# First cross attention: the next unit's scores follow the last mix, the final turn and half of the maxima come behind them

## The reference

```python
q = _split_heads(x @ wq.T + bq, H)
k = _split_heads(mem @ wk.T + bk, H)
v = _split_heads(mem @ wv.T + bv, H)
scores = jnp.einsum('bhqd,bhkd->bhqk', q, k) * (1.0 / math.sqrt(hd))
attn = jax.nn.softmax(scores, axis=-1)
out = _merge_heads(jnp.einsum('bhqk,bhkd->bhqd', attn, v))
```

## Time and profile before

| what | us |
|---|---|
| median of three runs | 3806.73 (3805.34 to 3807.47) |
| the profiled execution, its own time | 3805.49 |
| the profiled execution, span of its instructions | 3803.7 |
| first cross attention, from about 300 to about 1195 of the span | about 895 |

### The profile page before, as it was taken

How to read it: one execution, slowest core, us unless ns; L and a number is a source line. 1 busy time by engine, 2 the same in 40 slices (tenths; PEclk the granted TensorE clock), 3 DMA queues, 4 the chain that set the end, 5 groups by cost and what they waited for, 6 DMA issues and landing times. The chain is left out here.

```text
span 3803.7 us, 68033 instructions
## 1 busy us (share of the span) xinstructions
PE 3376.3 (89%) x26619; PEld 1977.6 (52%) x26619; DVE 2561.0 (67%) x5544; ACT 1947.0 (51%) x2681; POOL 1538.7 (40%) x1207
## 2 busy tenths in 40 slices
PE   5769999999997579599999999999999999779998
PEld 3555665666654367344444444444444444555555
DVE  3447777777775443488888888888888887464333
ACT  3325666666665412466666665665666665432222
POOL 1013333333330000176666667667666666310000
PEclk8768999999998769799999999999999999888999
DMA  1003333333330000201111101111110110001000
GB/s 53 1 26 80 69 75 78 72 79 72 75 71 15 0 24 1 66 18 35 35 35 35 35 20 33 35 35 35 35 35 18 35 35 9 1 11 60 1 1 12
DMA packets 90496, 139.23 MB, mean 37 GB/s; under 512 B 14464, under 2 KB 67776, under 8 KB 89408
## 3 DMA queue, kind: packets, MB, share of 16 engines
q1 hardware_dynamic: 90176, 134.87, 13.1%
HBM read 94.41 MB, written 1.05 MB: 25 GB/s over the span
## 5 line engine op out<-in xcount | busy, mean ns | idle before, releaser
L1899 PE MATMUL banks<-arena 128*128 128x512 f32 x1664 | 805.0, 604 | 3.0 <-ACT arena L2088 3.0
L2081 ACT ACTIVATE arena<-banks,arena 128x512 f32<-128x512 f32 x832 | 555.7, 685 | 468.8 <-PE banks L1874 468.8
L1833 POOL TENSOR_TENSOR arena<-arena 128x1024 f32<-128x1024 f32 x256 | 603.1, 2356 | 251.9 <-ACT arena L2088 251.0
L1080 DVE TENSOR_REDUCE arena<-banks 128x1 f32<-128x512 f32 (+1 forms) x896 | 529.8, 628 | 189.6 <-PE banks L965 184.4
L1177 ACT ACTIVATE arena<-banks 128x1024 f32<-128x1024 f32 (+1 forms) x448 | 425.1, 964 | 317.1 <-PE banks L986 314.2
L1983 DVE TENSOR_TENSOR banks<-arena,banks 128x512 f32<-128x512 f32 x640 | 443.2, 692 | 194.4 <-ACT arena L2081 180.3
L2000 DVE TENSOR_TENSOR arena<-arena,banks 128x1024 f32<-128x1024 f32 (+1 forms) x448 | 507.8, 1135 | 12.7 <-PE banks L1889 12.2
L2088 ACT ACTIVATE arena<-arena 128x1024 f32<-128x1024 f32 (+1 forms) x448 | 443.9, 991 | 117.1 <-DVE arena L2000 116.8
L1899 PEld LDWEIGHTS banks<-arena 128*128 128x128 f32 x1664 | 290.1, 190 | 223.2 <-issue 195.1
L1873 PE MATMUL banks<-arena 128*128 128x512 bf16 x832 | 316.3, 380 | 0.0
L1872 PE MATMUL banks<-arena 128*128 128x512 bf16 x832 | 316.0, 380 | 0.0
(11 more groups left out here) (345 smaller groups left out, 5505.6 us busy)
## 6 DMA issues: line engine op xcount, KB each, us to landing
arena<-in_ctxT SPq DMA_DIRECT2D x64, 800.5 KB, 5.6
arena<-arena SPq DMA_DIRECT2D x768, 50.0 KB, 2.2
arena<-in_ctx SPq DMA_DIRECT2D x32, 768.0 KB
arena<-in_m2w SPq DMA_DIRECT2D x3, 2048.0 KB, 12.5
arena<-in_xw SPq DMA_DIRECT2D x1, 2048.0 KB, 8.0
weights<-in_weights SPq DMA_DIRECT2D x1, 1918.0 KB, 7.6
arena<-in_ctx SPq DMA_DIRECT2D x32, 32.5 KB
arena<-in_m1w SPq DMA_DIRECT2D x1, 1024.0 KB, 6.3
```

Source lines behind the costliest of these rows:

```text
L1080: eng.tensor_reduce(o, s, AX, ALU.max).then_inc(a_max, 1)
L1833: eng.tensor_tensor(part, part, tiles, ALU.add).then_inc(sums, 1)
L1899: eng.matmul(c.ps[:, R_MIX + v % 2, :], ctxn[:, b, kt * D:(kt + 1) * D], st[:, v % 2, kt, :], start=kt == 0, stop=kt == KT - 1).then_inc(m ...
L2081: eng.activation(st[:, v % 2, kt, :], c.ps[:, n % SB, :], ACT.Identity, bias=hide[:, kt, v // 2:v // 2 + 1])\
```

## The change

PE: `maxima(v+2, 0)` moves from ahead of the mix of step 5 to behind `shifts`; `maxima(v+2, 1)`, `queries` and `final(v-1)` move from ahead of their mixes to behind the scores 0 and 1 of the next unit, in the order final, maxima, queries. DVE: the copy L1099 moves ahead of the maxima 0, and the two instructions of `final` move from step 4 to step 6, between the maxima 0 and 1. No instruction is added or removed, and ACT, POOL and SP are unchanged.

```diff
@@ PE body @@
                 for st in range(STEPS):
-                    if st < 5:
-                        if here(1):
-                            maxima(*later(i, v, 1), st + 2)
-                    elif here(2):
-                        maxima(*later(i, v, 2), st - 5)
+                    if st < 5 and here(1):
+                        maxima(*later(i, v, 1), st + 2)
...
-                    elif st == 4:
-                        if i + v > 0:
-                            final(*later(i, v, -1))
-                    elif st == 6 and v % 2 == 1 and more:
-                        queries(i + 1, v // 2)
                     mix(i, v, st)
                     if st < 5:
                         scores(i, v, st + 2)
-                    if st == 5 and here(1):
-                        shifts(*later(i, v, 1))
+                    if st == 5:
+                        if here(1):
+                            shifts(*later(i, v, 1))
+                        if here(2):
+                            maxima(*later(i, v, 2), 0)
                 if here(1):
                     scores(*later(i, v, 1), 0)
                     scores(*later(i, v, 1), 1)
+                if i + v > 0:
+                    final(*later(i, v, -1))
+                if here(2):
+                    maxima(*later(i, v, 2), 1)
+                if v % 2 == 1 and more:
+                    queries(i + 1, v // 2)
@@ DVE body @@
-                    if st < 5:
-                        if here(1):
-                            maxima(*later(i, v, 1), st + 2)
-                    elif here(2):
-                        maxima(*later(i, v, 2), st - 5)
+                    if st < 5 and here(1):
+                        maxima(*later(i, v, 1), st + 2)
                     if st == 4 and here(1):
                         spread_max(*later(i, v, 1))
-                    if st == 4 and old:
-                        final(*later(i, v, -1))
                     if st == 5 and here(1):
                         add_shift(*later(i, v, 1))
+                    if st == 6 and old:
+                        final(*later(i, v, -1))
+                    if st >= 5 and here(2):
+                        maxima(*later(i, v, 2), st - 5)
```

## The result

The changed kernel takes 3900.74 us (median of four, 3898.86 to 3905.98) against 3806.03: **94.7 us slower, a ratio of 1.0251 (1.0233 to 1.0268)**. The forecast was 3850 with a range up to 3866. The side was right and the size was not; the missing 51 us are the rival that was given 0.06.

What follows compares the result with a forecast made beforehand. PE was taken as the bound, idling a little. Even ends costing 1.06 us and odd ends 0.30, 31 each, plus 0.9 at the stage's end made 43.1 us more: 3850 us, range 3830 to 3866, rivals left out.

Steps and rivals of the forecast that it cites:

- What bounds the kernel: First cross attention: PE is the bound, idling a little; it waits about 1.0 us for late DVE reductions at even ends.
- Even unit, up to the scores: Step 4's mix to the next unit's scores: the scores come 1.77 us earlier, at 824.50 instead of 826.27.
- Even unit, behind the scores: Next unit's maxima wait for DVE reductions queued behind final's product; keys start at 828.29, not 827.23, costing 1.06 us.
- Odd unit: Odd unit's end: queries and then values wait for bank 7, values at 813.91 against 813.61, costing 0.30 us.
- The sum: 31 even ends at 1.06 and 31 odd at 0.30, plus 0.9 at the stage's end: 43.1 us, giving 3850.
- The 0.9 at the end of the stage: Unit 62's final between last mix and mask_mix: 1.5 us, less about 0.6 of PE work taken from step 4.
- The clock gives way: Rival: PE's longer idles lower the clock once per pair of units, 48 us more, 3898 us; chance 0.06.
- A rule to weigh: Final between scores and maxima changes tiling mode; a crossing costs 0.10 us, or 4 us more overall if each drained.
- Faster: Rival: banks 0 and 1 free in time, PE never stops behind the scores; 62 us gained, 3745 us; chance 0.05.
- no change: Rival: the odd end gains what the even end loses; 3806 us; chance 0.05.

Runs made afterwards that it cites:

- e1: The changed kernel plus unread matmuls where PE would idle, 20 in even units and 8 in odd: 3843.95 us, ratio 1.0106 to the kernel before.
- e8: The kernel before, with even units' final turn between maxima 1 and last mix on PE, behind maxima 1 on DVE: 3784.18 us, ratio 0.9954.

## Why the prediction was wrong in size

- **What bounds the kernel**: right. PE, with DVE late at the unit's end.
- **Even unit, up to the scores**: right. The last mix stands 10.38 us behind the first values (802.08 to 812.46); the working gives 823.94 - 813.61 = 10.33.
- **Even unit, behind the scores**: right, 4.36 us for 4.35. Moving scores forward gave PE nothing, for the very next instructions need banks that DVE empties last.
- **Odd unit**: right, 4.32 for 4.34. The bank 7 chain is as worked out.
- **The sum**: 43 us; e1 measures 41.9 against the kernel before of its own runs (34 to 47 by its interval). That it comes within about 1 us is in part luck: the order costs 44 where the sum has 42.2, and the sum does not take off the 5 us of lost clock that the kernel before had and e1 has not. The 0.9 at the end of the stage was not measured by itself. The term it lacks is the clock.
- **The clock gives way**: this is the step that failed. The forecast put the clock at nothing ("so I expect none") although it foresaw the idle of 1.4 us; the runs show 31.07 - 29.31 = 1.76 us a pair, 55 us in all. The rival's own price, once per pair, gave 3898 us, the result within 3, and that closeness is in part luck: it has 1.54 for 1.76, 7 us too little, and does not take off the 5 us that the kernel before already lost. Its chance, 0.06, rested on the last unit's 84% busy at a full clock: one stretch of 7.8 us that came once, not an idle of the same kind repeated in all pairs. And a warning stood in the rows: the kernel before lost the clock in the unit of the earlier trace rows, and in two more, with idle pieces of 0.2 us only, while the idle to come was 1.4 us in every pair. That such a kernel is near its edge is my reading; what set off its three stretches was not tested. The section "A second HAM failure mode: psum-queue depth-cycling" of the Trainium skill's TensorE: Matmul & The Clock Gate tells of a kernel in which PE idles for short moments between groups of matmuls, often enough that the clock swings between its two levels. The runs here agree with it: the stage's clock is 0.94 with the idle and 1.00 with it filled (e1).
- **A rule to weigh** (the tiling mode's drain): the row's price held. Scores to `final` took 0.56, as summed (813.02 to 813.58).
- **Faster** and **no change**: neither came. The second maxima matmul would have had to start by about 814.2, 0.5 us behind the scores' end; it started at 816.50.

## What to carry to other kernels

When work is pulled forward on the bounding engine, look at the instruction behind it: if that one needs a buffer which another engine frees in order, the wait moves and grows by what was put ahead of it on that other engine. In this kernel an idle piece of PE had two prices, one for its length (1.42 us a pair) and one for the clock (1.76), so weigh both, above all when the kernel before already loses the clock here and there; avoid such a gap by putting real work where PE would wait (e8) or, as a test, fill it with matmuls that nobody reads. A rival with the right price deserves a chance from rows with the same repeated pattern, not from a single stretch.

## What was not expected of the hardware

That PE could be given some 59 us more to do (1.29 us for 20 matmuls in the even unit and 0.6 for 8 in the odd one, in 31 pairs) and the kernel get 55 us faster was not expected. Nor that cutting the idle piece in two does not help: of 29 pairs in each trace, 1.16 us whole lose the clock in all and 0.34 with 0.75 in all but one. And the edge is sharp: 0.88 us of idle at the same place loses it in one pair of six.
